# Layer 1 of a graph network kernel: one group's sums in the middle of each step, two groups late

## The chip, the cores and the metric

The kernel runs on one core of one Trainium2 chip. The metric is the device time of an execution in microseconds. A core has five engines with an instruction stream each: TensorE (PE, matrix products), VectorE (DVE), ScalarE (ACT), GpSimd (POOL) and SyncE (SP), the last two here for DMAs. They work side by side and wait for one another through semaphores alone.

## The reference, cut to what matters

Two message passing layers over 12,500 nodes with 48 features and 200,000 edges that are sorted by their target node, each followed by a residual and a layer norm:

```python
# layer 0
h   = relu(concat([x[dst], x[src], edge_attr_32], 1) @ W1 + b1)
msg = h @ W2 + b2
x   = layernorm(x + segment_sum(msg, dst, 12500))
# layer 1
m   = relu(x[src] + edge_attr_48)
x   = layernorm(x + (1 + eps) * x + segment_sum(m, dst, 12500))
```

## The kernel before

**Groups and steps.** The edges are cut into 391 groups of 512: 4 tiles of 128 edges, one edge to a partition. Since targets are sorted, a group's targets lie in a window of 48 nodes. A step of layer 1 stands for one group; `i` counts fours of steps and `u` is 0 to 3 within one, so the group is `g = 4 * i + u`. All steps are written out, and each engine has its own order of them, in functions of the name `steps1`.

**A group's way through layer 1.** POOL gathers the rows `x[src]` of a group's tiles from DRAM with one indirect DMA each (line 561), four steps ahead. DVE adds the edge features (line 1137, `pre1`, which a view may call `edgeT`, the memory that it lies in). ACT takes the relu into the high part of the message (line 707), rounded to the type that PE multiplies; DVE writes what the rounding left as the low part (`low_part`, line 1037, semaphore `msg`). DVE also builds the one-hot rows that say to which of the 48 nodes each edge goes (`onehots`, line 1014, for the group after). PE then sums the messages of equal targets with four small matmuls, one for a tile, into `ps_s[g % 2]` (`sum_messages`, line 779, semaphore `seg`). The two halves of `ps_s` lie in one PSUM tile, `ps_as`. DVE adds the sums into the window of the table `acc` in SBUF (`accumulate`, line 1028, semaphore `acc`).

**The picks.** POOL would be too slow for all tiles, so for about three groups in four the fourth tile's rows are not gathered but picked by PE out of a copy of `x` in SBUF, in ten chunks of 1250 rows: a pick is ten chunks times two parts of the numbers, 20 matmuls of 480 columns (`pick_rows`, line 880). A list made in advance, `PRODUCTS`, gives each step its chunks: 8 in the steps up to the one at which the finished table begins to be normalised, 7 after it. A pick's one-hot matrix is built by DVE (`find_places`, line 1104, semaphore `places`, 1.9 steps or more before its first chunk), and its result is taken out by DVE (`select_rows`, lines 1113 and 1118, after the semaphore `ten`) in the first step in which the last chunk is done within 0.38 of the step. PE also counts thirds of each step's chunks (semaphore `third`); POOL issues the first three gathers of a group after the thirds of the step four before it, so that the gathers are spread.

**The order around the change.** PE, `steps1` in an even step: sums of the groups two and one back, one after the other; in some steps a piece of the finished table turned back into nodes (`to_nodes`); then the step's chunks. In an odd step: chunks only. The first group's sums wait for the accumulation of the group before it and for its message, the second group's for its message only. DVE, `steps1`: the sum of group `g`; one-hots of `g + 1`; in an even step the two accumulations, which wait for the later group's `seg`; the low part of `g`; the picks to be taken out; the places to be found; pieces of the normalisation. Layer 0 has an order of its own, which the change does not touch; its functions share `sum_messages` and `accumulate`.

Of the kernel before, what the change touches and what calls it, by code (L numbers as in the profile page):

```python
# [49 lines left out]
UNROLL = 4  # L50
WIN = 48
GROUPS = -(-E // GE)
# [78 lines left out]
PLAN, PRODUCTS = plan([(s, 10 if s < 0 else 8 if s < UNROLL * NORM_ITER else 7) for s in range(-AHEAD, GROUPS)], GROUPS - 1)  # L131
# [9 lines left out]
def build(nc, x, xT, src_tiles, dst_tiles, dst_groups, e32, e48, w1, w2, b1, b2, eps, ident, iota, center, normed,  # L141
          src_rows, src_columns, places, earlier, spare, out):
    ctx = ExitStack()
    with ctx:
# [201 lines left out]
        def wait_for(eng, s, g):  # L346

            if g >= 0:
                eng.wait_ge(s, g + 1)
# [8 lines left out]
        def is_group(i, u):  # L358
            return 0 <= i * UNROLL + u < GROUPS
# [402 lines left out]
        def _(pe):  # L762
# [9 lines left out]

            def sum_messages(S, g):

                if S is S1 and g % 2 == 0:
                    wait_for(pe, S["acc"], g - 1)
                wait_for(pe, S["msg"], g)
                for t in range(TILES):
                    last = nc.tensor.matmul(ps_s[g % 2], lhsT=msg[:, g % UNROLL, t, 0:SUMS], rhs=hot[:, g % UNROLL, t, :],  # L779
                                            start=(t == 0), stop=(t == TILES - 1))  # L780
                last.then_inc(S["seg"], 1)
# [75 lines left out]

            def steps1(i, u, c, before):

                if u % 2 == 0:  # L860
                    for back in (2, 1):
                        if is_group(i, u - back):
                            sum_messages(S1, i * UNROLL + u - back)
                if before is not None and u == 0:
                    pe.wait_ge(S1["staged"], before[0] + 1)
                    to_nodes(S1, staged, before)
                pick_rows(S1, PRODUCTS.get(i * UNROLL + u, ()), ps_picked)

            def pick_rows(S, products, banks):

                for q, c in products:
                    if c == 0:
                        if S is S0 and q > 0:
                            pe.wait_ge(S["picked"], 2 * q - 1)
                        pe.wait_ge(S["places"], q + 1)
                    for part in range(PARTS):
                        if part:
                            if (q, c) in (THIRDS0 if S is S0 else THIRDS):
                                last.then_inc(S["third"], 1)
                        last = nc.tensor.matmul(banks[q % len(banks)], lhsT=at_place[:, q % PLACED, c, :], rhs=x1_parts[:, c, part, :],  # L880
                                                start=(c == 0 and part == 0), stop=(c == CHUNKS - 1 and part == PARTS - 1))
                    if c == CHUNKS - 1:
                        last.then_inc(S["ten"], 1)
# [66 lines left out]
        def _(dve):  # L950
# [69 lines left out]
            def accumulate(S, g):  # L1020
                if g % UNROLL == 0:
                    starts[:] = first_nodes(dve, held, S["acc"].name, g // UNROLL)
                first = starts[g % UNROLL]
                if S is S1 or g % 2 == 1:
                    wait_for(dve, S["acc"], g - 1)
                if S is S1 and g % 2 == 0:
                    wait_for(dve, S["seg"], min(g + 1, GROUPS - 1))
                nc.vector.tensor_tensor(acc[0:SUMS, bass.ds(first, WIN)], acc[0:SUMS, bass.ds(first, WIN)], ps_s[g % 2], ALU.add).then_inc(S["acc"], 1)  # L1028

            def low_part(S, g):  # L1030
# [97 lines left out]
            def steps1(i, u, c, before):  # L1128

                if is_group(i, u):  # L1130
                    if i * UNROLL + u in PICK_OF:
                        dve.wait_ge(S1["picked"], 2 * PICK_OF[i * UNROLL + u] + 2)
                    if u % 2 == 0:
                        dve.wait_ge(S1["edges"][u // 2], i * 16 + 16)
                    g = i * UNROLL + u
                    dve.wait_ge(S1["rows"][g % RING], landed(S1, g))
                    nc.vector.tensor_tensor(pre1[:, u, :, :], edge[:, g % RING, :, D:2 * D], e48_sb[:, u, :, :], ALU.add).then_inc(S1["sum"], 1)  # L1137
                if is_group(i, u + 1):
                    onehots(g + 1, hot[:, (u + 1) % UNROLL, :, :], ps_iota)
                if u % 2 == 0:  # L1140
                    for back in (2, 1):
                        if is_group(i, u - back):
                            accumulate(S1, i * UNROLL + u - back)
                if is_group(i, u):
                    wait_for(dve, S1["high"], g)
                    low_part(S1, g)
                picks_of_step(i * UNROLL + u)
                if before is not None and u == 0:
                    add_residual(S1, before)
                if before is not None and u == 2:  # L1150
                    sum_squares(S1, before)
                if before is not None and u == 3:
                    divide(S1, before, in_resid(before), resid)
# [206 lines left out]
```

## Time and profile before

| what | us |
|---|---|
| median of 3 runs | 4178.44 |
| lowest and highest of them | 4169.53, 4180.32 |
| the profiled execution | 4175.66 |
| its span, first to last instruction | 4173.9 |
| granted TensorE clock, mean over the span | 0.883 |
| PE busy (share of the span) | 3670.4 (88%) |
| DVE busy | 2370.4 (57%) |
| POOL busy | 2628.5 (63%) |
| ACT busy | 750.7 (18%) |

The span is one execution as the hardware profiler saw it. "Busy" counts the time in which an engine has an instruction in work; matmuls overlap and their ends are modelled, so a PE that is busy all the time need not be at its peak. Layer 1's additions (line 1137) run from 2252.6 to 4159.6 us. A releaser, behind the arrow, is what ended an engine's idle time as far as semaphores tell; "issue" stands where nothing that was seen ended it, "remote" where the semaphore's update has no instruction that ends near it.

### The profile page before, as it was taken

Reading aid. Unit: us, or ns where it says so; the run is one execution under the profiler, and the core shown is the slowest. Engines: PE = TensorE matmul, PEld = TensorE weight load, DVE = VectorE, ACT = ScalarE, POOL = GpSimd, SP = SyncE. Lnnn points to the kernel's source line nnn. Section 1 sums busy time; section 2 is a strip of 40 time slices with the busy share of each in tenths; the row PEclk is TensorE's granted clock in tenths of the full one; section 3 lists DMA queues with packets and bytes.
Section 4 is the critical chain, followed back from the end, with each engine's and each line's share of the span. In section 5 each row is a group of like instructions: output and inputs, shape, how many; then the busy total and the mean of one; then the engine's idle time right before and its main releaser. Section 6 shows DMA issues by size and latency. Waiting matters only on the chain.

```text
span 4173.9 us, 54004 instructions
## 1 busy us (share of the span) xinstructions
PE 3670.4 (88%) x18202; PEld 3023.8 (72%) x18202; DVE 2370.4 (57%) x5096; ACT 750.7 (18%) x1666; POOL 2628.5 (63%) x2692
## 2 busy tenths in 40 slices
PE   4798898888898998899998888888888889888998
PEld 3576677677777777777786777777777777777876
DVE  3344444444444444444546777776777677776766
ACT  1222222222222222222331000000000000001111
POOL 6666666666666666666664666666666666666664
PEclk7688889889898898889998899999899999998887
DMA  5222222222222222222221222222222222222221
GB/s 103 33 34 35 34 34 36 34 34 36 34 35 35 34 35 35 34 34 40 38 37 41 46 49 48 49 49 46 48 48 49 46 49 48 49 48 48 51 52 43
DMA packets 408253, 178.47 MB, mean 43 GB/s; under 512 B 279196, under 2 KB 407138, under 8 KB 407874
## 3 DMA queue, kind: packets, MB, share of 16 engines
q0 software_dynamic: 86016, 66.23, 11.6%
q1 hardware_dynamic: 319778, 108.26, 11.3%
q8 instruction: 146, 2.39, 0.2%
q14 instruction: 135, 1.11, 0.1%
q10 hardware_dynamic: 2178, 0.48, 0.1%
HBM read 169.74 MB, written 5.00 MB: 42 GB/s over the span
## 4 chain that ended last, share of the span: by engine, by line
PE 18%; DVE 17%; issue 12%; another core or an unknown queue 10%; ACT 1%; DVEq 0%; DMA 0%; POOL 0%; POOLq 0%
PE ps_h L880 5%; DVE at_place L1104 5%; DVE picked L1113 5%; PE ps_t L880 4%; PE ps_early L880 2%; PE ps_as L779 2%; DVE edgeT L1137 2%; PE ps_out L787 1%; PE ps_h L838 1%; DVE msg L1037 1%; PE ps_nodes L890 1%; ACT msg L707 1%; DVE hot L1014 1%; DVE acc L1028 1%
## 5 line engine op out<-in xcount | busy, mean ns | idle before, releaser
L561 POOL DMA_INDIRECT edge<-x,resid_sb x1430 | 1421.7, 994 | 789.1 <-issue 404.9
L561 POOL DMA_INDIRECT edge<-x_dram,resid_sb x1258 | 1206.6, 959 | 731.0 <-issue 394.8
L880 PE MATMUL ps_h<-x_parts,at_place 125*128 125x480 f32 x3080 | 799.8, 416 | 33.2 <-issue 27.3
L1104 DVE TENSOR_TENSOR at_place<-place_row,ps_out 125x1280 fp32r<-125x1280 f32 x440 | 651.4, 1481 | 236.1 <-ACT msg L687 180.6
L880 PE MATMUL ps_t<-x_parts,at_place 125*128 125x480 f32 x3040 | 757.2, 404 | 20.4 <-issue 20.1
L880 PE MATMUL ps_early<-x_parts,at_place 125*128 125x480 f32 x2680 | 733.7, 423 | 31.4 <-DVE edge L1014 18.2
L880 PEld LDWEIGHTS ps_h<-x_parts,at_place 125*128 125x128 f32 x3080 | 640.6, 211 | 150.9 <-issue 43.4
L880 PEld LDWEIGHTS ps_early<-x_parts,at_place 125*128 125x128 f32 x2680 | 526.1, 198 | 230.8 <-issue 130.5
L880 PEld LDWEIGHTS ps_t<-x_parts,at_place 125*128 125x128 f32 x3040 | 602.2, 201 | 123.1 <-issue 30.2
L779 PE MATMUL ps_as<-hot,msg 128*97 128x48 f32 x3128 | 376.4, 254 | 244.8 <-DVE msg L1037 120.6
L779 PEld LDWEIGHTS ps_as<-hot,msg 128*97 128x97 f32 x3128 | 359.3, 181 | 287.8 <-DVE msg L1037 118.6
L838 PE MATMUL ps_h<-edgeT,w_edge 128*128 128x512 f32 x782 | 488.4, 757 | 18.3 <-DMA edge<-e 14.4
L787 PE MATMUL ps_out<-w_sb,hT 128*128 128x48 f32 x3128 | 474.0, 311 | 31.0 <-issue 27.7
L787 PEld LDWEIGHTS ps_out<-w_sb,hT 128*128 128x128 f32 x3128 | 452.1, 228 | 30.3 <-issue 26.6
L1057 DVE COPY w_edge<-ps_as 48x128 f32<-48x128 f32 x391 | 112.3, 287 | 602.7 <-remote 458.4
L707 ACT ACTIVATE msg<-edgeT 128x192 fp32r<-128x192 f32 x391 | 142.6, 365 | 1566.9 <-DVE edgeT L1137 912.9
L1028 DVE TENSOR_TENSOR acc<-acc,ps_as 97x48 f32 x782 | 159.8, 204 | 443.7 <-remote 337.3
L805 PE MATMUL ps_t<-ident_sb,edge 128*128 128x128 f32 x1564 | 228.0, 286 | 99.3 <-DMA edge<-x,resid_sb 66.9
L683 ACT ACTIVATE edgeT<-ps_t 128x512 f32<-128x512 f32 x391 | 219.8, 601 | 482.5 <-PE ps_t L805 206.6
L805 PEld LDWEIGHTS ps_t<-ident_sb,edge 128*128 128x128 f32 x1564 | 194.4, 149 | 142.9 <-DMA edge<-x,resid_sb 76.1
L1118 DVE TENSOR_REDUCE edge<-picked 128x48 f32<-128x480 f32 x440 | 287.4, 653 | 15.1
L1113 DVE SCALAR_TENSOR_TENSOR picked<-iota_sb,col_rest,ps_early 128x480 f32<-128x480 f32 x134 | 143.9, 1074 | 261.2 <-remote 112.8
(77 smaller groups left out, 2140.5 us busy)
## 6 DMA issues: line engine op xcount, KB each, us to landing
edgeT<-e SPq DMA_DIRECT2D x196, 192.0 KB
place_row<-rows_dram SPq DMA_DIRECT2D x440, 62.5 KB
edge<-e SPq DMA_DIRECT2D x196, 128.0 KB
edge<-x,resid_sb POOLq DMA_INDIRECT x1430
edge<-x_dram,resid_sb POOLq DMA_INDIRECT x1258
x_win<-xT SPq DMA_DIRECT2D x391, 9.0 KB
acc<-xT SPq DMA_DIRECT2D x10, 234.4 KB
feats<-x SPq DMA_DIRECT2D x10, 234.4 KB
```

The costliest lines, as they stand in the source:

```text
L561: pool.indirect_dma_start(out=cols, out_offset=None, in_=rows_of, in_offset=bass.IndirectOffsetOnAxis(ap=index, axis=0)).then_inc(done, 16)
L683: nc.scalar.activation(edgeT[:, g % UNROLL, :], ps_t[g % 2][:, :], ACT.Copy).then_inc(S0["edgeT"], 1)
L707: nc.scalar.activation(msg[:, u, :, 0:D], pre1[:, u, :, :], ACT.Relu).then_inc(S1["high"], 1)
L779: last = nc.tensor.matmul(ps_s[g % 2], lhsT=msg[:, g % UNROLL, t, 0:SUMS], rhs=hot[:, g % UNROLL, t, :], start=(t == 0), stop=(t == TILES ...
L787: last = nc.tensor.matmul(ps_m[:, g % 2, t, :], lhsT=hT[:, g % 2, t * P:(t + 1) * P], rhs=w2_sb[:, :], start=True, stop=True)
L805: last = nc.tensor.transpose(ps_t[g % 2][:, t * P:(t + 1) * P], edge[:, g % RING, t, :], ident_sb[:, :])
L838: nc.tensor.matmul(ps_h[g % 2][:, :], lhsT=w_edge[:, g % UNROLL, :], rhs=edgeT[:, g % UNROLL, :], start=True, stop=True).then_inc(S0["pre" ...
L880: last = nc.tensor.matmul(banks[q % len(banks)], lhsT=at_place[:, q % PLACED, c, :], rhs=x1_parts[:, c, part, :], start=(c == 0 and part = ...
L1028: nc.vector.tensor_tensor(acc[0:SUMS, bass.ds(first, WIN)], acc[0:SUMS, bass.ds(first, WIN)], ps_s[g % 2], ALU.add).then_inc(S["acc"], 1)
L1104: nc.vector.tensor_tensor(at_place[:, q % PLACED, :, :], place_row[:, q % PLACED, :].unsqueeze(1).to_broadcast([NP, CHUNKS, P]), ps_places ...
L1113: nc.vector.scalar_tensor_tensor(picked[:, :, :].rearrange("p f k -> p k f"), iota_sb[:, 0:CB].unsqueeze(2).to_broadcast([P, CB, D]), col_ ...
L1118: nc.vector.tensor_reduce(edge[:, group % RING, TILES - 1, D:2 * D], picked[:, :, :], AX.X, ALU.add).then_inc(S["picked"], 1)
```

## The change

PE puts the sums of one group, the one two back, in the middle of every step's chunks: first half of the chunks, four sums, second half. Each group's sums now wait for the accumulation of the group before. DVE accumulates one group in each step, the one two back, and does so after the low part of the step's own group in place of before it; each accumulation waits for its own group's sums.

```diff
             def sum_messages(S, g):
-                if S is S1 and g % 2 == 0:
+                if S is S1:
                     wait_for(pe, S["acc"], g - 1)
                 wait_for(pe, S["msg"], g)
...
             def steps1(i, u, c, before):          # PE
-                if u % 2 == 0:
-                    for back in (2, 1):
-                        if is_group(i, u - back):
-                            sum_messages(S1, i * UNROLL + u - back)
+                products = PRODUCTS.get(i * UNROLL + u, ())
+                pick_rows(S1, products[:len(products) // 2], ps_picked)
+                if is_group(i, u - 2):
+                    sum_messages(S1, i * UNROLL + u - 2)
                 if before is not None and u == 0:
                     pe.wait_ge(S1["staged"], before[0] + 1)
                     to_nodes(S1, staged, before)
-                pick_rows(S1, PRODUCTS.get(i * UNROLL + u, ()), ps_picked)
+                pick_rows(S1, products[len(products) // 2:], ps_picked)
...
             def accumulate(S, g):
-                if S is S1 and g % 2 == 0:
-                    wait_for(dve, S["seg"], min(g + 1, GROUPS - 1))
+                if S is S1:
+                    wait_for(dve, S["seg"], g)
...
             def steps1(i, u, c, before):          # DVE
                 if is_group(i, u + 1):
                     onehots(g + 1, hot[:, (u + 1) % UNROLL, :, :], ps_iota)
-                if u % 2 == 0:
-                    for back in (2, 1):
-                        if is_group(i, u - back):
-                            accumulate(S1, i * UNROLL + u - back)
                 if is_group(i, u):
                     wait_for(dve, S1["high"], g)
                     low_part(S1, g)
+                if is_group(i, u - 2):
+                    accumulate(S1, i * UNROLL + u - 2)
                 picks_of_step(i * UNROLL + u)
```

## Rows read from the trace of the kernel before

Columns of windows: the stretch, its length, then busy time and count for PE, PE's weight loads, DVE, ACT and POOL, granted clock, DMA share and GB/s. Groups: line, engine, operation, tiles, shapes, count | busy us, mean ns | idle before. Timelines: start, length, engine, line, operation, and in brackets the idle time before it with its releaser.

**Rows 1.** The page: busy time of each engine over the span.
```profile
PE 3670.4 (88%) x18202; PEld 3023.8 (72%) x18202; DVE 2370.4 (57%) x5096; ACT 750.7 (18%) x1666; POOL 2628.5 (63%) x2692
```

**Rows 2.** Windows: busy time of each engine in layer 1's steady stretch, granted clock.
```profile
2280.00:4160.00 1880.00, 1669.56 (x7725) 1422.23 (x7723) 1343.97 (x2512) 160.82 (x430) 1184.05 (x1235) 0.90 0.23 48
```

**Rows 3.** Groups by line and shape, 2280 to 4160 us.
```profile
L561 POOL DMA_INDIRECT edge<-x_dram,resid_sb x1235 | 1184.9, 959 | 685.2 <-issue 353.3 <-PE ps_h L880 134.3 <-PE ps_t L880 97.4
L880 PE MATMUL ps_h<-x_parts,at_place 125*128 125x480 f32 x3001 | 778.4, 416 | 27.5 <-issue 26.3
L880 PE MATMUL ps_t<-x_parts,at_place 125*128 125x480 f32 x3000 | 746.9, 404 | 16.5 <-issue 16.2
...
L779 PE MATMUL ps_as<-hot,msg 128*97 128x48 f32 x1544 | 182.7, 247 | 164.6 <-DVE msg L1037 117.8 <-issue 44.5 <-DVE acc L1028 1.7
...
L1137 DVE TENSOR_TENSOR edgeT<-edge,edgeT 128x192 f32<-128x192 f32 x386 | 136.6, 354 | 0.2
```

**Rows 4.** Timeline of PE, 3119 to 3142 us: two paired sums and the products between.
```profile
3120.21 0.79 PE L779 MATMUL ps_as<-hot,msg 128*97 128x48 f32 x8
3120.84 7.28 PE L880 MATMUL ps_h<-x_parts,at_place 125*128 125x480 f32 x32
3127.96 0.79 PE L779 MATMUL ps_as<-hot,msg 128*97 128x48 f32 x8
```

**Rows 5.** Timeline of POOL: the gathers around 3103 us.
```profile
3103.10 0.94 POOL L561 DMA_INDIRECT edge<-x_dram,resid_sb  x1 [0.30 <-issue]
3106.90 1.00 POOL L561 DMA_INDIRECT edge<-x_dram,resid_sb  x1 [2.85 <-PE ps_t L880]
```

**Rows 6.** Waits of PE and DVE, 2280 to 4160 us: total, times, longest.
```profile
DVE acc L1028 <- remote: 337.3, 70, 9.0
...
PE ps_as L779 <- DVE msg L1037: 117.8, 60, 4.0
...
PE ps_as L779 <- issue: 44.5, 46, 3.6
...
DVE acc L1028 <- PE ps_as L779: 39.1, 28, 2.9
```

**Rows 7.** Timeline of PE, 3098 to 3112 us.
```profile
3099.69 0.79 PE L779 MATMUL ps_as<-hot,msg 128*97 128x48 f32 x8
...
3103.92 3.68 PE L880 MATMUL ps_t<-x_parts,at_place 125*128 125x480 f32 x16
3107.44 0.44 PE L779 MATMUL ps_as<-hot,msg 128*97 128x48 f32 x4
3111.26 0.52 PE L779 MATMUL ps_as<-hot,msg 128*97 128x48 f32 x4 [3.38 <-DVE msg L1037]
```

**Rows 8.** Timeline of DVE, 3098 to 3112 us.
```profile
3098.56 0.35 DVE L1014 TENSOR_TENSOR hot<-ps_out,rel 128x192 fp32r<-128x192 f32 x1
3106.27 0.54 DVE L1028 TENSOR_TENSOR acc<-acc,ps_as 97x48 f32 x2 [7.36 <-remote]
...
3106.99 1.08 DVE L1113 SCALAR_TENSOR_TENSOR picked<-iota_sb,col_rest,ps_h 128x480 f32<-128x480 f32 x1
...
3108.67 1.48 DVE L1104 TENSOR_TENSOR at_place<-place_row,ps_out 125x1280 fp32r<-125x1280 f32 x1
...
3110.85 0.36 DVE L1037 SCALAR_TENSOR_TENSOR msg<-edgeT,msg 128x192 fp32r<-128x192 f32 x1 [0.16 <-issue]
```

**Rows 9.** Timeline of PE, 3088 to 3094 us.
```profile
3088.07 0.18 PE L779 MATMUL ps_as<-hot,msg 128*97 128x48 f32 x1 [1.17 <-issue]
3089.67 0.85 PE L779 MATMUL ps_as<-hot,msg 128*97 128x48 f32 x4 [1.42 <-DVE msg L1037]
3090.35 3.55 PE L880 MATMUL ps_t<-x_parts,at_place 125*128 125x480 f32 x8
3093.69 4.62 PE L880 MATMUL ps_h<-x_parts,at_place 125*128 125x480 f32 x17
```

**Rows 10.** Windows: the seven microseconds after those stops.
```profile
3088.00:3095.00 7.00, 5.51 (x17) 4.56 (x17) 6.34 (x15) 1.10 (x3) 4.12 (x5) 0.53 0.23 51
```

## The prediction

> **What bounds the kernel now.** The page comes first: TensorE (PE) is busy 88% of the span, ahead of every other engine [rows 1]. The change touches layer 1 only, so I take the stretch from 2280 to 4160 us, in which the paired accumulations begin and end: 1880 us for 386 steps (the count of the additions in line 1137), 4.87 us a step [rows 2, 3]. PE is busy 1670 us of it, VectorE (DVE) 1344, GpSimd (POOL) 1184; the granted clock is 0.90, and since it has only the levels 1.0 and 0.5, a fifth of the stretch, some 376 us, ran at 1.2 GHz [rows 2].
>
> Next the groups by line. The 6001 products of line 880 are 15.5 a step [rows 3]; at full clock 32 of them take 7.12 us, 0.222 each [rows 4], and a round of two steps (32 products and eight small matmuls of line 779) takes 7.75 us: the sums start at 3120.21 and again at 3127.96, the products at 3120.84 [rows 4]. So PE alone needs 3.87 us a step. DVE's idle share is 29%. POOL needs 1235 gathers at 0.96 us with 0.30 between them, 1556 us of the 1880, so it is the next floor, 320 us below [rows 2, 3, 5]. What is lost against 3.87 us a step are stops and half clock. The waits say where PE stops: in front of line 779, 117.8 us in 60 waits for DVE's message and 44.5 us in 46 that no releaser explains [rows 6]; in front of line 880 only 44 us (27.5 and 16.5) [rows 3]. The other side of the loop is DVE: before `accumulate` it stood 337.3 us in 70 waits whose releaser is "remote" and 39.1 us in 28 that PE's sums ended, longest 9.0 [rows 6].
>
> The timeline tells what "remote" is. PE's eight sums end at 3099.69 + 0.79 = 3100.48, but DVE, idle since 3098.91, starts the accumulation they release only at 3106.27: the signal came 5.8 us after the recorded end, while PE ran its 32 products meanwhile [rows 7, 8]. From there DVE needs two accumulations, a low part, a pick and an `at_place` (3106.99 to 3110.15, 3.2 us), the next sum, one-hots and the next low part, which ends at 3111.21: 4.94 us [rows 8]. PE, done with the first four sums at 3107.88, stands 3.38 us for that message [rows 7]. POOL sees the same lateness: it stood 2.85 us for a product's signal and went on at 3106.90 [rows 5].
>
> The Trainium skill bears on this: "Perfetto Trace Analysis", Tensor Engine Instruction, says the profiler computes a matmul's end from its size, and that PSUM's acknowledgement and the semaphore's spreading come after it, outside of the record. It names no price. If that tail were short and always the same, the first rival below would hold; a start 5.8 us after the end says it is neither.
>
> **The change part by part.** It computes nothing new. (1) Removed: at the head of every other step PE no longer needs the message of the step just before, so the 4.94 us chain leaves the loop. (2) Added: PE's four sums of group k-2 stand in the middle of step k, and each needs the accumulation of group k-3, which itself needs the sums in the middle of step k-1. Before, only even groups asked for that, and got it from a round earlier. So a signal must go from PE to DVE and back within each step. Behind PE's waiting sum stand the second half of the products and everything later; on them wait POOL's gathers (the thirds) and DVE's picks.
>
> How late may a signal come before PE stops? Before: from the end of eight sums to the point where the newer message is needed is 3107.88 - 3100.48 = 7.40 us, minus 4.94 is 2.4 us; the check is 5.8 - 2.4 = 3.4 for 3.38 seen. After: 3.87 less 0.35 for the four sums (half of 0.71, the sums' share of a round) less 0.35 for one accumulation of 0.20 and its hand-over: about 3.1 us. The allowance grows by 0.7 us, but it is tried every step instead of every second one.
>
> What that is worth depends on how long the late spells are. If a spell lasts S and starts anywhere in the loop, the first sums that fall in it at u see a lateness of S - u. With u even over 7.75 us the old stop is (S - 2.4)^2 / 15.5; with u even over 3.87 the new one is (S - 3.1)^2 / 7.74, and S - 5.04 where S is over 7.0. For S = 5.8 (the event above) 0.75 us before, 0.94 after; for 9.0 (the longest wait) 2.8 and 4.0. The ratio is 1.25 and 1.4. The stops in front of line 779 sum to 164 us now (117.8 + 44.5 and 1.7 more) [rows 3, 6]. Times 1.25 that is +41 us, times 1.4 +66. Below, if the late spells come with the paired sums and no more often than the 98 waits of today, 0.7 us more allowance saves 98 x 0.7 = 69 us, and if the wait for the message was all there was, 118 us. Above, doubling the places where PE can stop with 3.1 instead of 2.4 of 5.8 allowed is 164 x 2 x 2.7/3.4 = 260, +96. I take +41, since 5.8 us is the event that the rows show in full.
>
> (3) The clock. At half clock eight products take 3.34 us, 0.417 each, so 376 us at half clock cost 376 x (1 - 0.222/0.417) = 176 us. Those stretches follow PE's stops, and short ones are enough: 1.17 and 1.42 us of idle up to 3089.67 are followed by 0.53 of the clock from 3088 to 3095 [rows 9, 10]. If half clock goes with the time stopped, +41 of 208 us (164 + 44) is +35; single stops will be shorter than 3.4, so I take +15, with 0 to +80 as bounds (the last from +96).
>
> (4) Small things. Two groups of four sums interrupt the products twice in a round where one of eight did: one interruption costs 0.63 us from 3120.21 to 3120.84 for eight matmuls of 0.09; I put the second one at 0.02 each, 193 x 0.02 = 4 us (bounds -4 and +19, which is 0.1 each). DVE gets one more wait and one more separate accumulation in a round: nothing to 0.1 us each beside 29% of idle time, cost 0; if DVE ran with no idle time it would be 19 us. PE gets about 195 more separate wait instructions (one for each odd group), which its sequencer meets ahead of the products: 0, at most the same 19 us. Low part before accumulation in DVE's step: the message comes earlier and nothing waits for it, 0. The picks: `select_rows` now stands behind an accumulation that waits for the middle of PE's step; its bank is full in the first 0.38 of the step by the plan, so the middle comes last. 0 here; it is a rival below. No DMA moves.
>
> Sum: 4175.7 (profiled, 4173.9 of span and 1.8 around it) + 41 + 15 + 4 = 4236 us. The profiled time is 2.8 us under the median of the runs, within their spread, so I leave it: 4236.
>
> **The rivals.** A, the other side: the late signals do not depend on how often PE asks, and the wait for the message was the cost. Place: front of line 779. For it: 60 waits name DVE's message, and 0.7 us more allowance at each of 98 late waits is 69 us; with as much clock as goes with it at 0.85 us for one us stopped (176/208), less than half of it counted, 30 us: 4077. If all 118 us go and 50 of the clock, 4008. It decides when late spells last under about 5 us or end as soon as PE stops: at S = 5 the old stop is 0.44 and the new 0.47. Against it: 5.8 here, and a wait of 9.0 elsewhere.
>
> B, no change: shorter single stops, but more, and the clock balances the rest; 4165 to 4190. For it: both formulas lie close at 5 us.
>
> C, the picks become late. `find_places` is finished 0.35 + 0.2 + 3.2 us after the middle of PE's step, and the earliest product that needs it stands at least 1.9 to 2.0 steps after that step's head: 1.4 x 3.87 = 5.4 minus 3.45 leaves 1.95 us, in about a quarter of the picks. 1.15 us less than 3.1 at 98 late waits is 28 us for a quarter, 113 if each meets one: 4264 to 4349. Against it: line 880 waits only 44 us today.
>
> **How the numbers follow.** Forecast 0.37 (its own range 4195 to 4290), C 0.13, A 0.36, B 0.14. A measurement of this kernel tells 0.3% from no change. B is the chance of same; A that of faster; the forecast and C make slower 0.50. The range runs from 4060, which leaves out the quarter of A beyond it, to 4320, which holds the forecast with its upper bounds and the lower half of C.
>
> **What would show it.** Right: PE's waits in front of line 779 named DVE's accumulation (line 1028) instead of its message, more than 164 us in sum, single ones 1 to 3 us; DVE's waits before 1028 about twice as many; granted clock under 0.90 in layer 1. Rival A: line 779's idle time under 100 us and the clock over 0.90. C: idle time in front of line 880 well over 44 us with `at_place` as releaser. The forecast fails if signals late by 4 us or more become rare once PE stops for them in each step.

## The result, and the profile after

| | us | runs |
|---|---|---|
| before | 4178.0 (4169.53 to 4181.67) | 14 |
| after | 4189.14 (4181.32 to 4204.01) | 14 |
| ratio | 1.0034, interval 1.0025 to 1.0044 | |
| profiled execution | before 4175.66, after 4197.2 | |

The kernel is slower by 11 us in the medians, and by 0.34% in the ratio, which goes by the means of the runs. The forecast was 4236: its direction holds, its size doesn't, and the time lies within the range. Layer 1 (first to last addition of line 1137) took 1907.0 us before and 1913.4 after; the rest of the 21 us between the two profiled executions lies in layer 0 (layer 1 began at 2252.6 and at 2266.2), which the change doesn't touch.

The page of the kernel after, busy times, against [rows 1]:

```profile
PE 3638.2 (87%) x18202; PEld 2979.4 (71%) x18202; DVE 2375.8 (57%) x5096; ACT 751.9 (18%) x1666; POOL 2604.1 (62%) x2692
```

Windows of the kernel after, the stretch of [rows 2]. PE is busy 26 us less for the same work, and the granted clock is 0.92 where it was 0.90:

```profile
2280.00:4160.00 1880.00, 1643.27 (x7693) 1372.19 (x7693) 1345.99 (x2500) 159.33 (x426) 1173.94 (x1235) 0.92 0.23 48
```

Groups by line of the kernel after, against [rows 3]. The last column is the one to read: idle time in front of line 779 went from 164.6 to 226.1 us, and in front of line 880 from 44.0 to 11.1:

```profile
L561 POOL DMA_INDIRECT edge<-x_dram,resid_sb x1235 | 1174.3, 951 | 707.4 <-issue 346.5 <-remote 159.4 <-PE ps_h L880 109.5
L880 PE MATMUL ps_t<-x_parts,at_place 125*128 125x480 f32 x2990 | 768.5, 410 | 8.4 <-issue 6.5 <-DVE at_place L1104 1.9
L880 PE MATMUL ps_h<-x_parts,at_place 125*128 125x480 f32 x3000 | 756.6, 405 | 2.7 <-issue 2.7
...
L779 PE MATMUL ps_as<-hot,msg 128*97 128x48 f32 x1533 | 191.2, 244 | 226.1 <-DVE acc L1028 184.2 <-issue 39.0
```

Waits of DVE and PE, 2280 to 4160 us (total, times, longest), against [rows 6]. The releaser of line 779 is now DVE's accumulation, as forecast, and DVE's late signals before line 1028 are more, 116 for 70, but take only 53 us more in sum. PE's waits for it are 2.1 us long on average (184.2 in 86), where those for the message were 2.0 (117.8 in 60):

```profile
DVE acc L1028 <- remote: 390.8, 116, 8.3
...
DVE acc L1028 <- PE ps_as L779: 34.8, 23, 3.2
...
PE ps_as L779 <- DVE acc L1028: 184.2, 86, 7.5
PE ps_as L779 <- issue: 39.0, 36, 6.4
```

One late signal in full, PE and then DVE. PE's sums end at 3001.76 + 0.44 = 3002.20; the accumulation that they release starts at 3009.15, 6.95 us later; PE has run its 16 products and stands 3.60 us. So it was covered for 6.95 - 3.60 = 3.35 us; the prediction's allowance was 3.1.

```profile
3001.76 0.44 PE L779 MATMUL ps_as<-hot,msg 128*97 128x48 f32 x4
3002.04 3.77 PE L880 MATMUL ps_t<-x_parts,at_place 125*128 125x480 f32 x16
3009.41 0.85 PE L779 MATMUL ps_as<-hot,msg 128*97 128x48 f32 x4 [3.60 <-DVE acc L1028]
```

```profile
3002.93 0.36 DVE L1037 SCALAR_TENSOR_TENSOR msg<-edgeT,msg 128x192 fp32r<-128x192 f32 x1 [0.16 <-issue]
3009.15 0.21 DVE L1028 TENSOR_TENSOR acc<-acc,ps_as 97x48 f32 x1 [5.86 <-remote]
```

An undisturbed stretch of PE in the kernel after (timeline of run e10): three steps of 16 products take 3030.15 - 3018.50 = 11.65 us, 3.88 a step, 7.77 a round of two, where [rows 4] have 7.75.

```profile
3018.50 0.44 PE L779 MATMUL ps_as<-hot,msg 128*97 128x48 f32 x4
3018.79 3.76 PE L880 MATMUL ps_h<-x_parts,at_place 125*128 125x480 f32 x16
3022.39 0.45 PE L779 MATMUL ps_as<-hot,msg 128*97 128x48 f32 x4
...
3030.15 0.45 PE L779 MATMUL ps_as<-hot,msg 128*97 128x48 f32 x4
```

**Layer 1 as a sum.** From the trace I took every interval between two neighbouring starts of matmuls in layer 1, and split it into the pace of an undisturbed stretch, what half clock adds to it, and the rest, over 0.3 us (stops) or under (small waits). Each column is the pair on one chip; the second and third are runs e9/e10 and e15/e14.

| us in layer 1 | before, after | e9, e10 | e15, e14 |
|---|---|---|---|
| stops over 0.3 us | 242.3, 264.9 | 236.9, 251.9 | 52.6, 25.1 |
| of them ahead of sums | 181.1, 250.8 | 199.6, 232.6 | 52.6, 22.5 |
| added by half clock | 136.0, 105.8 | 114.3, 97.2 | 17.1, 19.6 |
| undisturbed pace and small waits | 1526.9, 1541.0 | 1526.4, 1540.9 | 1517.9, 1541.8 |
| layer 1 (with small remainders) | 1907.0, 1913.4 | 1879.2, 1891.9 | 1589.3, 1588.5 |
| time at half clock | 382, 283 | 321, 256 | 41, 48 |

("Time at half clock" is how long the granted clock stood at 1.2 GHz; "added by half clock" is what that cost.) So the change moves three things: stops +22.6 (+15.0 on the second chip), half clock -30.2 (-17.1), small waits and pace +14.1 (+14.5).

### The profile page after: what moved, and what is told of

Its sections match the earlier page's. It is cut to its first block, busy times and chain, and to the rows that moved or that the text cites. A ratio compares the mean times of both kernels' runs of the same rounds, so it can differ in the third digit from the quotient of the medians.

```text
span 4195.3 us, 54394 instructions
## 1 busy us (share of the span) xinstructions
PE 3638.2 (87%) x18202; PEld 2979.4 (71%) x18202; DVE 2375.8 (57%) x5096; ACT 751.9 (18%) x1666; POOL 2604.1 (62%) x2692
## 4 chain that ended last, share of the span: by engine, by line
PE 27%; DVE 25%; another core or an unknown queue 23%; issue 17%; ACT 3%; POOL 2%; DMA 1%; DVEq 1%; SPq 0%; POOLq 0%; ACTq 0%
DVE at_place L1104 9%; DVE picked L1113 7%; PE ps_early L880 7%; PE ps_out L787 5%; PE ps_h L838 4%; PE ps_as L779 3%; PE ps_h L880 3%; PE ps_t L880 3%; PE ps_t L805 2%; DVE edgeT L1137 2%; POOL edge L561 2%; DVE acc L1028 1%; DVE hot L1014 1%; DVE msg L1037 1%
## 5 line engine op out<-in xcount | busy, mean ns | idle before, releaser
L561 POOL DMA_INDIRECT edge<-x,resid_sb x1430 | 1407.5, 984 | 812.0 <-issue 400.0
L880 PE MATMUL ps_t<-x_parts,at_place 125*128 125x480 f32 x3040 | 779.6, 410 | 8.4 <-issue 6.5
L880 PE MATMUL ps_h<-x_parts,at_place 125*128 125x480 f32 x3080 | 778.3, 405 | 7.3 <-DVE x_parts L1195 4.6
L779 PE MATMUL ps_as<-hot,msg 128*97 128x48 f32 x3128 | 393.6, 255 | 338.9 <-DVE acc L1028 188.6
L779 PEld LDWEIGHTS ps_as<-hot,msg 128*97 128x97 f32 x3128 | 372.5, 182 | 432.4 <-DVE acc L1028 228.5
L880 PEld LDWEIGHTS ps_h<-x_parts,at_place 125*128 125x128 f32 x3080 | 599.5, 201 | 97.5 <-DVE x_parts L1195 4.8
L838 PE MATMUL ps_h<-edgeT,w_edge 128*128 128x512 f32 x782 | 475.7, 739 | 18.6 <-DMA edge<-e 14.2
```

The lines of the kernel that those rows point to most:

```text
L561: pool.indirect_dma_start(out=cols, out_offset=None, in_=rows_of, in_offset=bass.IndirectOffsetOnAxis(ap=index, axis=0)).then_inc(done, 16)
L838: nc.tensor.matmul(ps_h[g % 2][:, :], lhsT=w_edge[:, g % UNROLL, :], rhs=edgeT[:, g % UNROLL, :], start=True, stop=True).then_inc(S0["pre" ...
```

## The experiments

Sixteen experiments ran, in four groups, each group on a chip of its own. The kernel before took 4176.3, 3551.9, 4128.0 and 3549.5 us on them, so ratios are compared and never times of two groups. The second and fourth chip are a kind of their own, as will be seen. A "spell" below is a stretch in which PE's signals arrive late.

### First chip (before 4176.3 us): where the wait sits

**e1_pairs_late.** The kernel before, with its pairs taken three and two groups back, and DVE's accumulations moved ahead of its one-hots, so that the accumulation and both messages are older when PE asks.

```diff
-                    for back in (2, 1):
+                    for back in (3, 2):          # PE, sums; and DVE, accumulations, now ahead of the one-hots
```

> Paired sums at the head of every other step as before, but of the groups three and two back, so that PE never needs the message of the step just before; the question to DVE is asked once in two steps, as before. Theory 1 (allowance): what costs is how late a signal from PE to DVE may come before PE stops; here that is 7.1 us from the end of the sums to the next head less about 0.6 for two accumulations, 6.5 us, against 2.4 before and 3.1 after. PE's idle time in front of line 779 under 60 us (164 before, 228 after), time 4020 to 4110 us. Theory 2 (number of questions and the split cost, the message wait hides beside something else): within 10 us of before, 4178, with the stops moved to another line.

Measured 4169.41 us, 0.998 (0.997 to 0.999). The stops ahead of the sums fell to 34.8 us, as the allowance says, but 185.6 us of stops appeared ahead of the products, where there had been 60.9. The sum of stops is 227.3 against 242.3. So the 4020 to 4110 us of theory 1 did not come, and the time is within the 10 us of theory 2.

**e2_head_of_each.** The kernel after, with the group's sums at the head of the step.

```diff
-                pick_rows(S1, products[:len(products) // 2], ps_picked)
                 if is_group(i, u - 2):
                     sum_messages(S1, i * UNROLL + u - 2)
...
-                pick_rows(S1, products[len(products) // 2:], ps_picked)
+                pick_rows(S1, products, ps_picked)
```

> As after, but each step's sums stand at the head of the step's chunks and not amid them. The allowance is the same, 3.1 us, asked every step. Theory 1: like after, 4180 to 4200 us, about 230 us of idle time in front of line 779. If it is the place amid the chunks that took the stops in front of the products away (44 us before, 11 after) and kept the clock up, those stops come back and the time is 20 to 40 us above after.

Measured 4186.11 us, 1.0021 (1.001 to 1.0033). Stops 250.8, half clock 109.0 us: like the kernel after. The place in the step is worth about a tenth of a per cent, if anything: the intervals overlap.

**e3_own_bank.** The kernel after, with the odd groups' sums in another bank (free in layer 1 until the last groups), so that a group waits for the accumulation two groups back.

```diff
                 if S is S1:
-                    wait_for(pe, S["acc"], g - 1)
+                    wait_for(pe, S["acc"], g - (2 if g < OWN_BANK else 1))
...
-                    last = nc.tensor.matmul(ps_s[g % 2], ...
+                    last = nc.tensor.matmul(sums_of(S, g), ...
```

> As after, but the odd groups' sums of layer 1 (below group 376) go to a PSUM bank of their own, so that PE's sums wait for the accumulation of the group two back in place of one back. A signal may be 7.0 us late (two steps of 3.87 less 0.35 and 0.35) and is asked for every step, amid the chunks. Theory 1: idle time in front of line 779 under 60 us, time 4030 to 4120 us. Theory 2 (questions, split and DVE's order cost): like after, 4189.

Measured 4176.64 us, 1.0004 (0.9994 to 1.0013). Neither theory gave this time. It takes the change's loss away, but not the stops: 28.3 us of them are left ahead of the sums and 221.6 stand ahead of the products. The timeline of PE in one such spell, line 885 here being 880 of before: with nothing to wait for that the trace shows, PE starts one product at 3057.65, 3058.36, 3059.07 and 3059.78, one every 0.71 us, where it takes 0.22 otherwise. The signal of the sums before these, which ended at 3052.97, reached DVE only at 3062.78.

```profile
3052.53 0.44 PE L784 MATMUL ps_early<-hot,msg 128*97 128x48 f32 x4
...
3056.37 0.45 PE L784 MATMUL ps_as<-hot,msg 128*97 128x48 f32 x4
3056.66 0.68 PE L885 MATMUL ps_t<-x_parts,at_place 125*128 125x480 f32 x2
3057.65 0.38 PE L885 MATMUL ps_t<-x_parts,at_place 125*128 125x480 f32 x1 [0.30 <-issue]
3058.36 0.47 PE L885 MATMUL ps_t<-x_parts,at_place 125*128 125x480 f32 x1 [0.34 <-issue]
3059.07 0.38 PE L885 MATMUL ps_t<-x_parts,at_place 125*128 125x480 f32 x1 [0.24 <-issue]
3059.78 0.48 PE L885 MATMUL ps_t<-x_parts,at_place 125*128 125x480 f32 x1 [0.32 <-issue]
```

```profile
3062.78 0.21 DVE L1033 TENSOR_TENSOR acc<-acc,ps_early 97x48 f32 x1 [7.88 <-remote]
```

**e4_acc_first.** The kernel after, with DVE's accumulation ahead of the low part again.

```diff
+                if is_group(i, u - 2):
+                    accumulate(S1, i * UNROLL + u - 2)
                 if is_group(i, u):
                     wait_for(dve, S1["high"], g)
                     low_part(S1, g)
-                if is_group(i, u - 2):
-                    accumulate(S1, i * UNROLL + u - 2)
```

> As after, but DVE accumulates before it writes the low part of the step's own group. Nobody waits for that low part before two steps later. Theory 1: only where DVE itself is behind does the accumulation come 0.4 to 0.5 us earlier: 0 to 15 us faster than after. If DVE's order was a cost of the change, the time is back at before's 4178 or below, with less idle time in front of line 779 than 228 us.

Measured 4187.82 us, 1.0031 (1.0019 to 1.0043), the same as the kernel after: the half microsecond of DVE's order doesn't matter.

After these four, the picture was: every version has 227 to 265 us of stops in layer 1; the order decides only in front of which line they stand. And the versions with eight sums in a row (before, e1) spent 382 and 358 us at half clock, those with four (after, e2, e3, e4) 273 to 283.

### Second chip (before 3551.9 us): parts left out

All four expectations were written in times of the first chip; read them as ratios.

**e5_one_part.** The kernel after, with the second part of each product of layer 1 left out and no thirds counted there; its picked rows come out less exact.

```diff
-                    for part in range(PARTS):
+                    for part in range(PARTS if S is S0 else 1):
```

> Leaves work out: layer 1's picks multiply the first part of the numbers alone (10 products a pick in place of 20), and POOL's gathers of layer 1 do not wait for thirds; all else as after. PE then needs about 2.1 us a step and gets half the instructions. In e3 the stops came back in front of the products without a releaser, single products 0.71 us apart, so theory 3 says that PE is not supplied with instructions during the late spells, and that total stops are given by these spells and not by who is waited for. If the spells come with the number of PE's instructions (some 140 apart in the traces so far), they are half as many here: layer 1 runs at POOL's and DVE's pace, 1600 to 1680 us, time 3870 to 3950. If they come with time (every 16 us), DVE still loses about 350 us to late signals: 4000 to 4100.

Measured 3540.31 us, 0.9963 (0.9947 to 0.9978).

**e6_no_thirds.** The kernel after, without the thirds of layer 1: POOL no longer waits for PE's signals.

```diff
-                            if (q, c) in (THIRDS0 if S is S0 else THIRDS):
+                            if S is S0 and (q, c) in THIRDS0:
...                                                  # POOL
-                if step >= 0 and t < 3 and thirds_of(PRODUCTS.get(step, ())):
-                    pool.wait_ge(S1["third"], thirds_before(PRODUCTS, step) + t + 1)
+                return
```

> As after, but layer 1's products signal no thirds and POOL's gathers do not wait for them (the ring of eight groups still holds POOL back). PE sends 1167 less signals. If the late spells are the price of many signals, PE's stops fall from 265 us to under 150 and the time to 4100 or less. Theory 3 (supply of instructions): stops unchanged within 30 us, time 4175 to 4200.

Measured 3547.56 us, 0.9986 (0.9976 to 0.9997).

**e7_pair_split.** The kernel before, with the even step's second group of sums amid the step's chunks: four sums in a row in place of eight, nothing else.

```diff
                 if u % 2 == 0:
-                    for back in (2, 1):
-                        if is_group(i, u - back):
-                            sum_messages(S1, i * UNROLL + u - back)
+                    if is_group(i, u - 2):
+                        sum_messages(S1, i * UNROLL + u - 2)
+                    pick_rows(S1, products[:half], ps_picked)
+                    if is_group(i, u - 1):
+                        sum_messages(S1, i * UNROLL + u - 1)
...
-                pick_rows(S1, PRODUCTS.get(i * UNROLL + u, ()), ps_picked)
+                pick_rows(S1, products[half:], ps_picked)
```

> As before, but of the two groups' sums in an even step the second stands amid that step's chunks and not right behind the first. Half clock in layer 1 was 382 and 358 us in the two kernels with eight sums in a row and 273 to 283 in the four with four in a row. If the row of eight is what lowers the clock, half-clock time falls to about 280 here; if it is the message wait or how often DVE is asked, it stays at 350 or more. Theory 3: all of PE's stops together stay at 240 to 260 us, since the message wait only takes the place of stops that the supply would make; time 4160 to 4178. Theory 1: the message may come 1.8 us later, stops in front of the sums fall from 181 to about 90 and the time by as much.

Measured 3548.5 us, 0.9986 (0.9975 to 0.9998).

**e8_late_split.** e1 with the split of e7: the group three back at the head, the one two back amid the chunks. The cut shows the difference from e7 on PE.

```diff
-                    if is_group(i, u - 2):
+                    if is_group(i, u - 3):
...
-                    if is_group(i, u - 1):
+                    if is_group(i, u - 2):
```

> As e1 (groups three and two back, asked once in two steps), with the second group's sums amid the even step's chunks. Theory 3: PE's stops together 220 to 250 us as in e1; with the half clock at 280 in place of 358 us the time is 4150 to 4165, the fastest of all. If the clock stays at 350, it is like e1, 4169.

Measured 3548.32 us, 0.9986 (0.9976 to 0.9996).

None of the four told what it was made for, since there was nothing on this chip to move: stops in layer 1 were 27 to 40 us, time at half clock 38 to 58 us (e5 apart, in which PE has half its work in products and is idle for 395 us before sums and products from 1960 to 3510 us, 591 us of layer 1 being at half clock). But these four traces have no late spells, and those of the first chip all have, so the spells look like a property of the chip; the third and fourth chip, with both kernels unchanged, test that.

### Third chip (before 4128.0 us): spells again

**e9_before_again** and **e10_after_again** are the two kernels as they are.

> The kernel before, unchanged, for a trace beside its own kind on the same chip; 1.000 is expected by all. The open point: the chips differ. On the first one (kernel before 4176 us) PE's signals arrive late in spells every 15 to 18 us and the engine is supplied with one matmul per 0.71 us in them; on the second (kernel before 3552 us) the traces of four experiments show no such spell. If this chip is of the second kind, the trace of this kernel should show in layer 1 stops ahead of PE's sums and products of 30 to 60 us in all, in place of 243, under 60 us of layer 1 at half clock in place of 382, and no waits put down to a remote releaser on POOL; if of the first kind, the old numbers within 10%.

> The kernel after, unchanged, beside the kernel before on the same chip. Theory 3 (the late spells set how long PE stops in layer 1, and the order of the sums only sets where): on a chip without spells there is nothing to move, and what is left of the change is the small gaps it adds between products and the one wait more per group: ratio 0.998 to 1.001. Rival (one wait per step has a price of its own in DVE's order, spells or not, as the prediction's allowance says): ratio 1.002 to 1.004 there too, with stops ahead of the sums above those of the kernel before by 15 us or more. On a chip of the first kind both expect 1.0034 again (1.0025 to 1.0044).

Measured 1.0001 (0.9987 to 1.0014) for the kernel before, and 4143.07 us, 1.0036 (1.0023 to 1.0049), for the kernel after. The result repeats on a second chip with spells. Groups by line from 2280 to 4130 us, first e9, then e10: ahead of line 779 the idle time rises by 32 us and ahead of line 880 it falls by 14.

```profile
L880 PE MATMUL ps_h<-x_parts,at_place 125*128 125x480 f32 x2979 | 744.5, 405 | 12.6 <-issue 12.2
L880 PE MATMUL ps_t<-x_parts,at_place 125*128 125x480 f32 x2960 | 741.1, 406 | 11.5 <-issue 11.4
...
L779 PE MATMUL ps_as<-hot,msg 128*97 128x48 f32 x1532 | 181.0, 246 | 184.9 <-DVE msg L1037 104.0 <-issue 79.3 <-DVE acc L1028 0.9
```

```profile
L880 PE MATMUL ps_h<-x_parts,at_place 125*128 125x480 f32 x2968 | 760.6, 409 | 1.3 <-issue 1.3
L880 PE MATMUL ps_t<-x_parts,at_place 125*128 125x480 f32 x2960 | 741.1, 402 | 8.9 <-DVE at_place L1104 6.3 <-issue 2.6
...
L779 PE MATMUL ps_as<-hot,msg 128*97 128x48 f32 x1536 | 190.2, 242 | 217.2 <-DVE acc L1028 177.8 <-issue 36.9
```

**e11_pair_split_again** is the kernel e7.

> The kernel before with the even step's two groups kept, but the second one's four sums amid the step's chunks, so that four sums stand in a row in place of eight and the allowance stays that of the kernel before. On a chip of the first kind: theory 4 (eight sums in a row bring PE to half clock, since every version with eight had 358 to 382 us of layer 1 at half clock and every one with four 273 to 283) expects 290 us or less at half clock and a ratio of 0.992 to 0.998; the rival (half clock follows the stops alone, whatever stands in a row) expects 350 to 390 us and a ratio of 0.998 to 1.002. On a chip of the second kind both expect 0.998 to 1.000, as it had there before.

Measured 4124.55 us, 0.9986 (0.9975 to 0.9998). Half clock 276 us against 321 in e9, which is what theory 4 expects and its rival doesn't (350 to 390); but the time saved is smaller than the 0.992 to 0.998 it gave. In the account of layer 1, half clock gave back 8.9 us and stops 8.5, and 9.7 went to pace and small waits. So four in a row instead of eight does bring less half clock, and is worth about a tenth of a per cent. Each trace is one execution, but the mean granted clock over all runs agrees: 0.892 for the kernel before on this chip (32 runs) and 0.897 for this one (12 runs).

**e12_own_bank_again** is the kernel e3.

> The kernel after with the odd groups' sums of layer 1 in a bank of their own, so that a group's sums wait for the accumulation two groups back. It takes away the wait for the last accumulation, which the change asks for at every group. On a chip of the second kind theory 3 expects the same as the kernel after there, within 0.1% (nothing to wait for either way), and the rival expects it to be faster than the kernel after by 0.3% (15 us of stops and the gaps behind them). On a chip of the first kind both expect 1.000 again, with the stops in front of the products.

Measured 4126.92 us, 0.9996 (0.9986 to 1.0007). Groups of e12, 2280 to 4130 us, lines five higher than before: the 217.2 us of e10 ahead of the sums are 32.8, and ahead of the products 160.6 in place of 10.2. Of these 160.6, 71.0 are waits for `at_place`: DVE brings it late, presumably held up itself by the late signal, so not every stop here is one without a releaser.

```profile
L885 PE MATMUL ps_t<-x_parts,at_place 125*128 125x480 f32 x2960 | 780.5, 411 | 112.7 <-DVE at_place L1109 64.3 <-issue 46.4
L885 PE MATMUL ps_h<-x_parts,at_place 125*128 125x480 f32 x2979 | 766.4, 406 | 47.9 <-issue 40.2 <-DVE at_place L1109 6.7
...
L784 PE MATMUL ps_as<-hot,msg 128*97 128x48 f32 x796 | 94.7, 238 | 16.8 <-DVE acc L1033 11.7 <-issue 5.1
L784 PE MATMUL ps_early<-hot,msg 128*97 128x48 f32 x740 | 87.8, 234 | 16.0 <-issue 16.0
```

Twice now the change without its wait for the last accumulation takes the time of the kernel before (1.0004, 0.9996), while with the wait it takes 1.0034 and 1.0036. The wait is what costs. The edit takes the other bank along with the wait; my account of stops, half clock and pace speaks for the wait, since layer 1 gets 12.9 us shorter from e10 to e12 with some 18 us of stops less, 6 us of half clock more, and pace and small waits within 5 us.

### Fourth chip (before 3549.5 us): both kernels without spells

**e13_late_split_again** is the kernel e8, **e14_after_third** and **e15_before_third** are the two kernels as they are, **e16_one_part_again** is the kernel e5.

> The kernel before with pairs of groups three and two back (as e1) and the pair's second group amid the even step's chunks (as e11): the version that the two point to together. Chip with late spells: if the two gains add up (0.9980 of e1 and 0.9986 of e11, the one from the allowance, the other from half clock), 0.995 to 0.998, with half clock in layer 1 under 300 us; if they are the same gain seen twice, 0.998 to 0.999. Chip without spells: 0.998 to 1.000, as it had there before.

Measured 3550.12 us, 0.9996 (0.9984 to 1.0009). Whether the gains of e1 and e11 add up on a chip with spells stays open: this kernel met none.

> The kernel after, unchanged. Chip with late spells: 1.0035 (1.0023 to 1.0049) a third time. Chip without: cause 1 (spells) expects 0.998 to 1.001, the 190 more changes from sums to products at 0.08 us being 15 us of PE's time that is no longer the bound in full, and stops ahead of the sums of 15 to 40 us in place of 233 to 251; cause 2 (the order itself) expects 1.002 to 1.004.

Measured 3551.27 us, 1.0001 (0.999 to 1.0012), as cause 1 expects.

> The kernel before, unchanged, one look for its trace beside the kernel after on this chip. Chip without spells: stops ahead of sums and products of layer 1 of 30 to 60 us and under 60 us at half clock by cause 1, over 150 us of stops by cause 2. Chip with spells: 228 to 265 us of stops and 320 to 380 us at half clock again.

One execution, 3555.35 us: 52.6 us of stops and 41 us at half clock, as cause 1 expects. Groups from 1960 to 3520 us, the gathers and the sums of e15 and then of e14. No "remote" is left on POOL, and none in DVE's waits either; PE's idle time ahead of the sums is 41.2 us before, 40.7 of it for the message, and 18.5 us after, 11.8 of it for the accumulation.

```profile
L561 POOL DMA_INDIRECT edge<-x_dram,resid_sb x1236 | 1183.9, 958 | 376.7 <-issue 296.2 <-PE ps_h L880 51.5 <-PE ps_t L880 26.5
...
L779 PE MATMUL ps_as<-hot,msg 128*97 128x48 f32 x1528 | 166.0, 237 | 41.2 <-DVE msg L1037 40.7
```

```profile
L561 POOL DMA_INDIRECT edge<-x_dram,resid_sb x1239 | 1183.7, 955 | 377.6 <-issue 261.5 <-PE ps_h L880 61.9 <-PE ps_t L880 39.0
...
L779 PE MATMUL ps_as<-hot,msg 128*97 128x48 f32 x1531 | 180.3, 236 | 18.5 <-DVE acc L1028 11.8
```

The same rows hold a warning: POOL's gathers and the 0.30 us between them fill the whole stretch (1183.9 + 376.7 = 1560.6 of 1560 us). On this chip POOL bounds layer 1, and a change in PE's order could not have shown much in either direction.

> The kernel after with the second of the two parts of every product of layer 1 left out (its picked rows come out less exact) and no thirds counted: 3000 matmuls and as many weight loads fewer, some 600 us of PE's busy time. Chip without spells: 0.996, as it had there. Chip with spells: if PE's matmul time bounds layer 1, it falls to what POOL or DVE allow, ratio 0.88 to 0.93; if spells of late signals bound it by themselves in every engine that waits for PE, the ratio is 0.95 to 0.99.

Measured 3540.87 us, 0.9969 (0.9959 to 0.9979). It confirms that bound: with half of PE's products gone only 0.3% is saved, and POOL again has no time left (1175.2 + 375.8 = 1551.0 of 1550, 1960 to 3510 us):

```profile
L561 POOL DMA_INDIRECT edge<-x_dram,resid_sb x1233 | 1175.2, 953 | 375.8 <-issue 370.9 <-DVE edgeT L1136 4.9
```

## Why the prediction was right in its direction and wrong in its size

- **What bounds the kernel** held. PE bounds layer 1 on the measured chip as far as the rows tell (POOL is idle there for some 315 us beyond the 0.30 us at each gather); halving PE's products, which would test it, ran only on chips without spells. POOL comes 320 us below it, and the chips without spells, which run that far down, end at POOL's floor: their 1589 us of layer 1 are 318 less than the 1907 here.
- **The new wait** held. In front of line 779 stands DVE's accumulation, the idle time rose, and the measured allowance is 3.35 us for 3.1. Its size was also about right at the line that it was worked out for: 164.6 us became 226.1, a factor of 1.37, between the 1.25 taken (+41) and the 1.4 of the longer spell (+66). Rival A (under 100 us at line 779) and rival C (`at_place` ahead of line 880: 1.9 us) didn't come. Rival C's allowance had a slip besides: 5.4 less 0.35 + 0.2 + 3.2 is 1.65 us and not 1.95; its path did open in e12, where PE waits 71.0 us for `at_place`. DVE's late waits became 139 (116 and 23) for 98, not twice as many.
- **Rival B**, no change, is where the number landed: 4189 lies in its 4165 to 4190, and that the clock balances the stops is half of what it said. Its other half, shorter single stops, didn't come (2.1 us for 2.0).
- **The step that failed in the sum of stops** is the sentence that PE stops in front of line 880 for 44 us, which I carried over unchanged. Those stops weren't a place of their own. In a spell PE seems to lose a certain time, first at whichever wait it meets; a stop for the accumulation lets the spell pass, and the products behind it find it over. That is argued from the sums of stops, 227 to 265 us in every version on the first chip. So 61.5 us more at line 779 came with 32.9 less at line 880, net +28.6 by the rows and +22.6 by the account of layer 1. e1, e3 and e12 show the reverse: without the wait ahead of the sums the products stop 186 to 222 us by the account.
- **The clock** failed most: +15 us forecast, -30 measured (-17 on the third chip), 45 of the 54 us by which the sum for layer 1 missed. "Half clock goes with the time stopped" was the wrong step. Stops rose and half clock fell, from 382 to 283 us. In the account stops of under 1.5 us were followed by half clock (begun within 1 us of their end) in 26 cases of 125 before and in 4 of 85 after; those over 2.8 us in 16 of 19 and 29 of 33. [rows 9, 10] show such a short one, beside sums. e11 shows that splitting eight sums into four is enough to bring half clock down (321 to 276 us). The short stops are not the link: by the same count they are 11 of 110 in e9 and 22 of 147 in e11, whose half clock is less, and 43 of 223 in e3 with the least half clock of its chip (273 us), but 45 of 194 in e1 with 358. What divides all versions with spells is the row of eight (321 to 382 us) or four sums (256 to 288), wherever the stops stand; why, the runs don't show.
- **Small things** were +4 and came to +14. The part that I worked out, 0.02 us for a second interruption in a round, measured 0.02 (7.75 to 7.77, 4 us over 193 rounds). The other 10 us are waits under 0.3 us, which I had put at 0 "beside 29% of idle time"; they are there without the wait for the last accumulation too (e3), and which instruction makes them no run separates. The upper bounds, 19 us each, held.
- **The sum**: forecast 41 + 15 + 4 = +60; layer 1 of the profiled pair 22.6 - 30.2 + 14.1 = +6.5 (measured +6.4), of the third chip 15.0 - 17.1 + 14.5 = +12.4 (measured +12.7), and medians of +11 and +15 us. In both pairs stops and clock alone come to less than nothing (-7.6 and -2.1); the small waits, put at +4, turn the sign. So the right direction was luck: two terms of the wrong size, +41 and +15, and one that was taken for almost nothing.

The cause in one sentence: on a chip with spells the change pays 0.35% for asking at every step for the accumulation of the step before, shown by e3 and e12 against the kernel after (the other bank that they need was not tried by itself). That rests on ratios of 1.0034 to 1.0004 and of 1.0036 to 0.9996. That the change without this wait comes out just at the time of the kernel before is a balance: less half clock against more small waits. Without spells it costs nothing, though there POOL would hide it.

The fastest version measured is e1 (0.998, interval 0.997 to 0.999), on one chip; e11 (0.9986) is the only other whose interval excludes no change on a chip with spells.

## What to carry to other kernels

Stops that come from outside the kernel's order (a late signal, a slow supply) are a quantity of time that is shared among waits: when a new wait takes more of it, look for the line that takes less, and price the sum, not the line. Don't let the price of half clock follow the time stopped: here it went with how many short matmuls stood in a row, eight or four, at nearly the same time stopped. Price small waits too: a term of +14 us put at +4 decided the sign. And before an order is tuned to a stall, see on a second chip whether the stall is there at all.

## What the runs showed of the hardware

- The kernel before takes 3550 us on two chips and 4128 to 4178 on the others. All the traces of the slower ones have spells in both layers, mostly 12 to 20 us apart, in which PE's signals arrive several us late (5.8, 6.95 and 9.8 us in the three events shown) and, in the one shown, PE starts one product per 0.71 us; no trace of the faster ones has any. Their interval is a count of the late bursts of PE's signals. The granted clock differs too, 0.95 for 0.88 to 0.90, but at 2.4 GHz the median undisturbed round of the kernel before takes 7.75 us on either kind, so in layer 1 it is the spells and what follows them that make the difference. Where they come from no run here shows.
- The Trainium skill ("Perfetto Trace Analysis", Tensor Engine Instruction) says that a matmul's end in the trace is computed and that its acknowledgement comes later. On a chip without spells nothing late is seen: DVE's waits before its accumulation are 51 us from 1960 to 3520 us in e14, none by a remote releaser. A lateness of 5.8 and 6.95 us is then more than that tail.
- On the chips without spells no stop was followed by half clock within 1 us (76 stops in e15, 56 in e14, all under 1.5 us); on the others some of the same length were (26 of 125, 4 of 85).
